# Mixture parts of a macaron block: gates of later blocks over the partitions by DMA through DRAM, rows normalised a block sooner

## The chip, the cores and the metric

One core of one Trainium2 chip runs the whole kernel. The time is the device time of an execution in microseconds (us). TensorE (PE) multiplies, VectorE (DVE), ScalarE (ACT) and GpSimd (POOL) do the rest, and SyncE (SP) issues all DMAs, in order.

## The reference, cut to what matters

The input x has 4 x 1024 rows of 256. Three sublayers follow each other: half a mixture, an attention with its own MLP, and half a mixture again with the same weights.

```python
x = x + 0.5 * _L0_ffn_ref(_layernorm(x), ...)
x = x + _L0_attn_ref(_layernorm(x), ...)
x = x + 0.5 * _L0_ffn_ref(_layernorm(x), ...)

def _L0_ffn_ref(x, gate_W, W1, b1, W2, b2, Ws1, bs1, Ws2, bs2, route_scale):
    scores = sigmoid(x @ gate_W) * route_scale
    topk_scores, topk_idx = top_k(scores, 2)
    topk_w = topk_scores / topk_scores.sum(-1, keepdims=True)
    gate_full = einsum('bsk,bske->bse', topk_w, one_hot(topk_idx, 8))
    h = gelu(einsum('bsd,edh->bseh', x, W1) + b1, approximate=False)
    y = einsum('bseh,ehd->bsed', h, W2) + b2
    shared = gelu(x @ Ws1 + bs1, approximate=False) @ Ws2 + bs2
    return einsum('bse,bsed->bsd', gate_full, y) + shared
```

There are 8 experts of width 128 and one shared one of the same width. Every expert is computed for every row; the gate multiplies its hidden layer.

## The kernel before, in words

The program has four parts: f (first mixture, and behind it the rows z for the attention, normalised twice and transposed, and the attention's weights, split in two), a (attention), m (the attention's MLP) and g (second mixture). f and g come out of one function, `ffn_phase`, with `tail` true for f. Each product in full precision is made of three of a high and a low part (`hi` on ACT rounds, `lo` on DVE takes what is left).

Both mixtures take the 4096 rows in NB = 8 blocks of BT = 512 (NT = 4 tiles of 128). The engines run their own lists in order, written out by hand in `body(i, par, first, last)` of each engine, and meet at counting semaphores. A block is a loop over e = 0 to 8, the steps: step 0 is the shared expert, steps 1 to 8 the gated ones. In a step

- PE makes the first layer (`first_layer`, L855, six products into `hid`), the gate product (`gate`, L873: `sel` picks one row of the transposed gates `gst` and spreads it over 128 partitions into `gbc`), and the second layer of the expert two steps back (`second_layer`, L896, twelve products into `acc`; at the first of a block also four products with the biases, L888);
- ACT makes the Gelu (`act_out`, L469), then `hi` of the expert before (L461);
- DVE makes `gated` = gate x `act_out` (`gating`, L670), then `lo` of the expert before (L676).

Between these stand, in block i, the pieces for block i + 1: statistics of its rows (`x_stats`), POOL's reciprocal root (`x_rstd`), `x_norm` to `xn`, its transposes (PE, L822, into the bank `aux`), `xt_hi` and `xt_lo`, the logits (L832), `neg_logits`, POOL's power for the sigmoid (`expneg`, L552), `choices` (the two largest) and `gates`, which lay the gates out in `gpad`. `gates_up` transposes `gpad` (L842) at step 0 of the next block, and `gate_stack` copies it into `gst`. In f there is also the work on the rows z of block i - 1: `z_stats` and `zz_stats` on DVE, two chains on POOL (`z_rstds`, L535 to L548), `z_norm` (L407, after step 4's Gelu) and `zn_norm` on ACT, transposes on PE, `zt_hi` and `zt_lo`.

In block 0 of f, ACT and DVE also split the attention's weights (`qkv_hi`, `qkv_lo`) into one buffer, `qkv_s`; SP stores it (`store_qkv`) before the next pair may be written. The code of block i on SP loads the rows for the residual, stores the results of block i - 1, loads the rows of block i + 2 and stores z of block i - 1.

## Time and profile before

| | |
|---|---|
| three runs | 2463.77, 2451.25, 2459.19 us; median 2459.19 |
| the profiled execution | 2457.1 us, span 2454.2 us |
| busy in the span | PE 98%, DVE 76%, ACT 69%, POOL 61% |
| f | from 0 to some 287 us |
| g | from some 2196 us to the end |
| mean granted clock of PE | 0.996 of 2.4 GHz |

The profile records one execution. The span is from its first to its last instruction; the execution's own time is 2.9 us more. Busy time of PE counts pipelined products, so what it waits for is read from its timeline, not from its share.

### The profile page before, as it was taken

The numbers are of one execution on the slowest core, as the hardware profiler recorded it, in microseconds if no ns is written. First come the engines' busy times: TensorE is split into PE (matmuls) and PEld (weight loads), VectorE is DVE, ScalarE is ACT, GpSimd is POOL, SyncE is SP. The second block draws the span as 40 slices with busy tenths as digits, with TensorE's granted clock in tenths as the row PEclk, the third lists the DMA queues.
The fourth block names the chain that finished last, engine by engine and source line by source line (L and its number), as shares of the span: only waits on it lengthen the run. The fifth ranks groups of instructions, "written<-read, shape, count | busy, mean of one in ns | idle before, by whom it ended". The sixth has DMA issues, their size and how long they took to land.

```text
span 2454.2 us, 46643 instructions
## 1 busy us (share of the span) xinstructions
PE 2405.0 (98%) x14568; PEld 2087.9 (85%) x14568; DVE 1862.3 (76%) x3599; ACT 1686.6 (69%) x2920; POOL 1505.2 (61%) x1536
## 2 busy tenths in 40 slices
PE   8999889999999999999999999999999999999999
PEld 7888778888888888888888888888888879988888
DVE  7777677878878788887878878788887865556665
ACT  4555577878778787777878778787877864543333
POOL 1333277787777777767777777777768754542220
PEclk9999999999999999999999999999999999999999
DMA  5422531223212132221213312132221345331111
GB/s 204 172 102 94 181 112 44 87 68 96 95 40 89 45 101 71 75 95 43 86 60 100 97 35 94 43 98 73 77 95 43 108 169 171 122 130 34 46 51 43
DMA packets 128311, 220.16 MB, mean 90 GB/s; under 512 B 6810, under 2 KB 89652, under 8 KB 119476
## 3 DMA queue, kind: packets, MB, share of 16 engines
q1 hardware_dynamic: 128180, 218.78, 27.6%
q8 instruction: 37, 0.61, 0.1%
q14 instruction: 94, 0.77, 0.1%
HBM read 114.95 MB, written 53.48 MB: 69 GB/s over the span
## 4 chain that ended last, share of the span: by engine, by line
PE 81%; DVE 8%; issue 6%; POOL 2%; ACT 2%; DMA 1%; SPq 0%; DVEq 0%; ACTq 0%; POOLq 0%
PE a_ov L1622 19%; PE a_sc L1586 18%; PE a_tr L1598 18%; PE a_pj L1541 7%; PE a_pj L1550 4%; PE g_acc L896 3%; PE g_hid L855 3%; PE f_acc L896 3%; PE f_hid L855 2%; PE m_proj L2025 1%; POOL m_zin L1877 1%; PE m_hid L2091 1%; DVE f_hp L676 1%; DVE g_hp L676 1%; PE g_aux L832 1%
## 5 line engine op out<-in xcount | busy, mean ns | idle before, releaser
L1498 DVE TENSOR_REDUCE a_nmax<-a_sc 128x1 f32<-128x1024 f32 x512 | 626.8, 1224 | 260.3 <-PE a_sc L1586 252.1
L1425 POOL TENSOR_SCALAR a_pr<-a_pr,a_rden 128x1024 f32<-128x1024 f32 x512 | 575.1, 1125 | 256.2 <-DVE a_rden L1503 185.7
L1341 ACT ACTIVATE a_pT<-a_tr 128x512 fp32r<-128x512 f32 x1024 | 559.8, 596 | 205.5 <-PE a_tr L1598 197.2
L1509 DVE TENSOR_TENSOR a_pT<-a_tr,a_pT 128x512 fp32r<-128x512 f32 x1024 | 650.1, 677 | 17.7 <-ACT a_pT L1341 17.7
L1622 PE MATMUL a_ov<-a_pT,a_v_s 128*128 128x512 f32 x2048 | 600.2, 415 | 3.1 <-DVE a_half L1489 2.0
L1347 ACT ACTIVATE a_pr<-a_sc,a_nmax 128x1024 f32<-128x1024 f32 x512 | 573.5, 1120 | 31.8 <-DVE a_nmax L1498 28.2
L1586 PE MATMUL a_sc<-a_k_s,a_q_s 128*128 128x512 f32 x2048 | 554.1, 392 | 3.4 <-DMA a_k_s<-a_k_s 3.4
L1598 PEld LDWEIGHTS a_tr<-f_ident,a_pr 128*128 128x128 f32 x4096 | 473.0, 140 | 93.6 <-DVE a_pT L1509 18.8
L1598 PE MATMUL a_tr<-f_ident,a_pr 128*128 128x128 f32 x4096 | 537.8, 273 | 9.8 <-DVE a_pT L1509 9.6
L1586 PEld LDWEIGHTS a_sc<-a_k_s,a_q_s 128*128 128x128 f32 x2048 | 380.0, 188 | 83.7 <-DMA a_k_s<-a_k_s 3.6
L1622 PEld LDWEIGHTS a_ov<-a_pT,a_v_s 128*128 128x128 f32 x2048 | 347.5, 189 | 54.3 <-issue 4.9
L1541 PE MATMUL a_pj<-a_z_s,a_wqk_s 128*128 128x512 f32 x756 | 193.6, 391 | 2.5 <-issue 2.2
L1541 PEld LDWEIGHTS a_pj<-a_z_s,a_wqk_s 128*128 128x128 f32 x756 | 141.6, 188 | 34.9 <-issue 3.3
L1302 ACT ACTIVATE a_staged<-a_pj,f_bias 128x512 f32<-128x512 f32 x126 | 86.8, 689 | 93.8 <-PE a_pj L1541 77.4
L469 ACT ACTIVATE g_act_out<-g_hid,f_b 128x512 f32<-128x512 f32 x72 | 49.6, 688 | 144.5 <-PE g_hid L855 144.5
L896 PEld LDWEIGHTS f_acc<-f_w2p,f_hp 128*128 128x128 f32 x864 | 114.0, 193 | 11.1 <-DVE f_hp L676 6.3
L469 ACT ACTIVATE f_act_out<-f_hid,f_b 128x512 f32<-128x512 f32 x72 | 49.2, 684 | 107.0 <-PE f_hid L855 107.0
L896 PE MATMUL f_acc<-f_w2p,f_hp 128*128 128x256 f32 x864 | 117.5, 286 | 4.5 <-DVE f_hp L676 3.9
L896 PEld LDWEIGHTS g_acc<-g_w2p,g_hp 128*128 128x128 f32 x864 | 112.1, 190 | 8.2 <-DVE g_hp L676 2.9
L896 PE MATMUL g_acc<-g_w2p,g_hp 128*128 128x256 f32 x864 | 115.5, 283 | 1.3 <-DVE g_hp L676 0.9
L855 PE MATMUL f_hid<-f_xT,f_w1p 128*128 128x512 f32 x432 | 115.7, 404 | 0.0
L855 PE MATMUL g_hid<-g_xT,g_w1p 128*128 128x512 f32 x432 | 113.1, 397 | 0.0
(222 smaller groups left out, 3260.0 us busy)
## 6 DMA issues: line engine op xcount, KB each, us to landing
a_z_s<-zT SPq DMA_DIRECT2D x32, 1024.0 KB, 7.8
a_k_s<-a_k_s SPq DMA_DIRECT2D x62, 512.0 KB, 5.7
a_wqk_s<-w_split SPq DMA_DIRECT2D x64, 256.0 KB, 3.2
a_v_s<-a_v_b SPq DMA_DIRECT2D x16, 1024.0 KB, 4.6
att<-a_ao SPq DMA_DIRECT2D x32, 512.0 KB, 2.9
m_in<-att SPq DMA_DIRECT2D x16, 1024.0 KB, 6.1
a_wv_s<-w_split SPq DMA_DIRECT2D x17, 512.0 KB, 3.8
zT<-f_zT SPq DMA_DIRECT2D x8, 1024.0 KB, 3.9
```

Source lines behind the costliest of these rows:

```text
L469: act.activation(act_out[:, e % 3], hid[:, (par + e) % 2], ACT.Gelu, bias=b1[:, weights_of(e):weights_of(e) + 1]).then_inc(s["gelu"], 1)
L855: o = pe.matmul(hid[:, (par + e) % 2], w1p[:, a, (c * NE + x) * HID:(c * NE + x + 1) * HID], xT[:, par, c, b], start=(n == 0), stop=(n == 5))
L896: o = pe.matmul(acc[:, t], hp[:, e % 3, a, t * P:(t + 1) * P], w2p[:, b, x * D:(x + 1) * D], start=False, stop=(e == NE - 1 and (a, b) == ...
L1341: act.activation(pT[:, (u // 4) % 2, 0, 4 * part:4 * part + 4, (u % 4) * P:(u % 4 + 1) * P], tr[:, part].rearrange("p (t q) -> p t q", t=4 ...
L1347: act.activation(pr[:, k % NP], sc[:, k % 2], ACT.Exp, bias=nmax[:, k % NP:k % NP + 1], accum_out=den[:, k % NP:k % NP + 1]).then_inc(s["e ...
L1425: pool.tensor_scalar(pr[:, k % NP], pr[:, k % NP], rden[:, k % NP:k % NP + 1], 1.0, ALU.mult, ALU.mult).then_inc(s["normed"], 1)
L1498: dve.tensor_reduce(nmax[:, k % NP:k % NP + 1], sc[:, k % 2], AX.X, ALU.max, negate=True).then_inc(s["negmax"], 1)
L1509: dve.tensor_tensor(to[:, 1], tr[:, part].rearrange("p (t q) -> p t q", t=4), to[:, 0].bitcast(F32), ALU.subtract).then_inc(s["tr_lo"], 1)
L1541: o = pe.matmul(bank[:], wqk_s[:, "QK".index(kind), c, a], z_s[:, c * 2 + b, part], start=(i == 0), stop=(i == 5))
L1586: o = pe.matmul(sc[:, k % 2, kb * BT:(kb + 1) * BT], q_s[:, slot, head, tile * P:(tile + 1) * P], k_s[:, slot, head, a, kb * BT:(kb + 1) * ...
L1598: o = pe.transpose(tr[:, part, j * P:(j + 1) * P], pr[:, (k - LAG) % NP, (4 * part + j) * P:(4 * part + j + 1) * P], ident[:])
L1622: o = pe.matmul(ov[:], v_s[:, vslot, kt, 2 * vhead:2 * vhead + 2] .rearrange("p k f -> p (k f)"), pT[:, blk % 2, a, kt], start=(kt == 0 an ...
```

## The change

It touches `ffn_phase` (both f and g). For blocks 1 to 7 the gate product is gone. `gpad` gets a fourth copy, of the unrounded gates at columns 64 to 71 (`EXACT`); after the transposes ACT copies these eight rows to `gf`, SP stores them to DRAM (`gate_rows`), waits for that, and loads them back spread over all partitions into `gB`, in two halves of four experts. `gating` reads `gB` there. Block 0 is gated as before.

For that, the gates of block i + 1 are ready within block i: from block 1 on the transposes of the rows stand in step 0 and the logits in step 1 (both in the free bank `gbc`), neg in step 2, choices in step 4, gates in step 5, `gates_up` in step 6, the copies in step 7 (tables `STEADY` and `FIRST`); and the rows of block i + 2 get their statistics in step 7 and are normalised in step 8. On POOL `expneg` comes ahead of both z chains. In f the rows of block 1 are loaded in the prologue and share a semaphore with the selector and the bias rows. Some semaphores are merged in the other parts, which leaves their orders as they were.

```diff
+    STEADY = dict(up_x=0, logits=1, neg=2, choices=4, gates=5, up_gates=6, gf=7, stack=7)
+    FIRST = dict(norm=2, up_x=3, logits=4, neg=5, choices=7, gates=7, up_gates=8, gf=8, stack=8) if tail else \
+        dict(stats=0, norm=1, up_x=2, logits=3, neg=4, choices=6, gates=7, up_gates=8, gf=8, stack=8)
...
+        def gates_across(i, counts):
+
+            copied, out, used = counts
+            half = E // 2
+            sp.wait_ge(s["gf"], copied)
+            sp.dma_start(gate_rows, gf[EXACT:EXACT + E]).then_inc(s["gates_out"], 16)
+            sp.wait_ge(s["gates_out"], out)
+            for h in range(2):
+                if h == 1:
+
+                    sp.wait_ge(s["gated"], used)
+                sp.dma_start(gB[:, h * half:(h + 1) * half].rearrange("p e t -> p (e t)"),
+                             gate_rows[h * half:(h + 1) * half].rearrange("e t -> (e t)").unsqueeze(0).partition_broadcast(P))\
+                    .then_inc(s["gates_in%d" % h], 16)
...
             if tail and has(i, -1):
                 store_z(i - 1, z_to)
+            if has(i, 1):
+                gates_across(i, counts)
...
+        def gate_copy(i, first):
+            act.wait_ge(s["gT_ps"], i + 1)
+            if not first:
+
+                act.wait_ge(s["gates_out"], (i - 1) * 16)
+            act.activation(gf[EXACT:EXACT + E], up_bank(first)[EXACT:EXACT + E, 0], ACT.Identity).then_inc(s["gf"], 1)
...
         def body(i, par, first, last):
-            if not last:
-                x_rstd(i + 1)
-            if tail and not first:
-                z_rstds(i - 1, 0)
+            if first and not tail:
+                x_rstd(1)
             if not last:
                 expneg(i + 1)
             if tail and not first:
+                z_rstds(i - 1, 0)
                 z_rstds(i - 1, 1)
+            if has(i, 2):
+                x_rstd(i + 2)
...
+        def gating(i, e, first):
             dve.wait_ge(s["gelu"], i * NE + e + 1)
-            dve.wait_ge(s["gbc"], i * E + e)
-            dve.tensor_tensor(gated[:, e % 3], gbc[:, (e - 1) % 2], act_out[:, e % 3],
-                              ALU.mult).then_inc(s["gated"], 1)
+            if first:
+                dve.wait_ge(s["gbc"], e)
+                gate = gbc[:, (e - 1) % 2]
+            else:
+                dve.wait_ge(s["gates_in%d" % ((e - 1) // (E // 2))], i * 16)
+                gate = gB[:, e - 1]
+            dve.tensor_tensor(gated[:, e % 3], gate, act_out[:, e % 3], ALU.mult).then_inc(s["gated"], 1)
...
         def gate(i, e, par, first):
 
-            if shared(e):
+            if shared(e) or not first:
                 return
```

SP's list at the end of block 0 of f, before (`w_split` is the store of the attention's weights, twice):

```order
L294 DMA f_qkv_in<-in_w_qkv 128x2048
L297 DMA f_xin<-in_x 128x4x256 [waits f_xn]
L360 DMA f_xres<-in_x 128x4x256
L366 DMA f_xin<-in_x 128x4x256 [waits f_xn]
L372 DMA w_split<-f_qkv_s 128x4096 [waits f_qkv_lo] x2
L360 DMA f_xres<-in_x 128x4x256 [waits f_res]
```

and now:

```order
L316 DMA f_qkv_in<-in_w_qkv 128x2048
L392 DMA f_xres<-in_x 128x4x256
L398 DMA f_xin<-in_x 128x4x256 [waits f_xn]
L364 DMA f_gate_rows<-f_gf 8x512 [waits f_gf]
L370 DMA f_gB<-f_gate_rows 128x2048 [waits f_gates_out]
L370 DMA f_gB<-f_gate_rows 128x2048 [waits f_gated]
L406 DMA w_split<-f_qkv_s 128x4096 [waits f_qkv_lo] x2
L392 DMA f_xres<-in_x 128x4x256 [waits f_res]
```

The three DMAs of the gates, the first and the second with waits of their own, have come ahead of both stores of the weights.

POOL's list in one block of the loop of f, before (`f_rs` is of the rows x, `f_zrs` and `f_zshift` of the rows z, `f_nl` is the power):

```order
L536 TENSOR_SCALAR f_rs<-f_mv 128x4 [waits f_stats]
L538 TENSOR_TENSOR f_rs<-f_rs,f_mhalf 128x4 [waits f_veps]
L532 ISA
L535 TENSOR_SCALAR f_zshift<-f_zmv 128x4 [waits f_z_stats]
L536 TENSOR_SCALAR f_zrs<-f_zmv 128x4
L538 TENSOR_TENSOR f_zrs<-f_zrs,f_mhalf 128x4 [waits f_z_veps]
L548 TENSOR_TENSOR f_zshift<-f_zshift,f_zrs 128x4 [waits f_z_rs]
L552 TENSOR_TENSOR f_nl<-f_ebase,f_nl 128x32 [waits f_neg]
```

and now:

```order
L595 TENSOR_TENSOR f_nl<-f_ebase,f_nl 128x32 [waits f_neg]
L575 ISA
L578 TENSOR_SCALAR f_zshift<-f_zmv 128x4 [waits f_z_stats]
L579 TENSOR_SCALAR f_zrs<-f_zmv 128x4
L581 TENSOR_TENSOR f_zrs<-f_zrs,f_mhalf 128x4 [waits f_z_veps]
L591 TENSOR_TENSOR f_zshift<-f_zshift,f_zrs 128x4 [waits f_z_rs]
L575 REGISTER_ALU
```

The power has gone from behind the first z chain to the head of the block; the rows of x have gone to its end.

PE's list in steps 6 and 7 of the loop of f now (`f_gpad` is what DVE's gate arithmetic writes):

```order
L919 MATMUL f_hid<-f_xT,f_w1p 128x512 [waits f_gelu]
L919 MATMUL f_hid<-f_xT,f_w1p 128x512 x5
L961 MATMUL f_acc<-f_w2p,f_hp 128x256 [waits f_h_lo]
L961 MATMUL f_acc<-f_w2p,f_hp 128x256 x11
L906 MATMUL f_gbc<-f_ident,f_gpad 128x128 [waits f_gpad]
L906 MATMUL f_gbc<-f_ident,f_gpad 128x128 x3
```

The transposes of the gates stood in step 0 of the next block, behind the whole block's other work.

## Rows read from the trace of the kernel before

**Rows 1.** Timeline of PE in f: start, us, line, operation, tile, count, idle before.
```profile
88.67 0.66 PE L842 MATMUL f_aux<-f_ident,f_gpad 128*128 128x128 f32 x4
...
101.86 1.63 PE L855 MATMUL f_hid<-f_xT,f_w1p 128*128 128x512 f32 x6
103.32 0.39 PE L873 MATMUL f_gbc<-f_gst,f_sel 128*128 128x512 f32 x1
103.55 1.59 PE L896 MATMUL f_acc<-f_w2p,f_hp 128*128 128x256 f32 x12
...
106.37 0.39 PE L873 MATMUL f_gbc<-f_gst,f_sel 128*128 128x512 f32 x1
...
121.22 0.65 PE L842 MATMUL f_aux<-f_ident,f_gpad 128*128 128x128 f32 x4 [0.20 <-DVE f_zT L718]
```

**Rows 2.** Timeline of PE in g.
```profile
2261.73 0.66 PE L842 MATMUL g_aux<-f_ident,g_gpad 128*128 128x128 f32 x4 [0.40 <-DVE g_gpad L661]
...
2293.44 0.66 PE L842 MATMUL g_aux<-f_ident,g_gpad 128*128 128x128 f32 x4 [0.39 <-DVE g_gpad L661]
```

**Rows 3.** Timeline of POOL in the same block of f.
```profile
103.12 0.20 POOL L535 TENSOR_SCALAR f_zshift<-f_zmv 128x4 f32<-128x4 f32 x1 [9.32 <-DVE f_zmv L581]
...
106.03 5.43 POOL L552 TENSOR_TENSOR f_nl<-f_ebase,f_nl 128x32 f32<-128x32 f32 x1 [1.02 <-DVE f_nl L610]
111.54 0.73 POOL L535 TENSOR_SCALAR f_zshift<-f_zmv 128x4 f32<-128x4 f32 x1
```

**Rows 4.** Timeline of ACT in the same block.
```profile
105.12 2.08 ACT L407 ACTIVATE f_zz<-f_res,f_zshift,f_zrs 128x256 f32<-128x256 f32 x4 [0.39 <-POOL f_zshift L548]
```

**Rows 5.** Timeline of DVE in the same block.
```profile
107.89 0.69 DVE L670 TENSOR_TENSOR f_gated<-f_gbc,f_act_out 128x512 f32<-128x512 f32 x1 [1.94 <-ACT f_act_out L469]
108.50 0.68 DVE L676 TENSOR_TENSOR f_hp<-f_gated,f_hp 128x512 fp32r<-128x512 f32 x1
109.10 1.40 DVE L576 BATCH_NORM_STATS2 f_zst<-f_zz 128x6 f32<-128x256 f32 x4
...
110.95 0.67 DVE L670 TENSOR_TENSOR f_gated<-f_gbc,f_act_out 128x512 f32<-128x512 f32 x1
...
114.68 0.17 DVE L627 TENSOR_SCALAR f_sg<-f_nl 128x32 f32<-128x32 f32 x1
...
117.05 0.69 DVE L670 TENSOR_TENSOR f_gated<-f_gbc,f_act_out 128x512 f32<-128x512 f32 x1 [0.21 <-DVE f_idx L636]
...
118.25 0.16 DVE L643 TENSOR_TENSOR f_ws<-f_top 128x4 f32<-128x4 f32 x1
...
120.41 1.28 DVE L718 TENSOR_TENSOR f_zT<-f_aux,f_zT 128x512 fp32r<-128x512 f32 x2
```

**Rows 6.** DMA issues: count, KB each, median us from issue to landing.
```profile
w_split<-f_qkv_s SPq DMA_DIRECT2D x3, 2048.0 KB, 6.5
...
z<-f_zz SPq DMA_DIRECT2D x8, 512.0 KB, 2.9
...
w_kept<-f_w2p SPq DMA_DIRECT2D x1, 2304.0 KB, 15.2
```

**Rows 7.** Timeline of PE in the last block of f.
```profile
271.91 2.38 PE L896 MATMUL f_acc<-f_w2p,f_hp 128*128 128x256 f32 x12 [2.63 <-DVE f_hp L676]
```

**Rows 8.** Timeline of PE at the start of block 1 of f.
```profile
52.78 0.66 PE L842 MATMUL f_aux<-f_ident,f_gpad 128*128 128x128 f32 x4 [1.99 <-DVE f_gpad L661]
...
57.04 2.77 PE L896 MATMUL f_acc<-f_w2p,f_hp 128*128 128x256 f32 x12
```

**Rows 9.** Timeline of ACT in the prologue and at the end of block 0.
```profile
12.35 0.42 ACT L501 ACTIVATE f_b2s<-f_b_in 128x256 fp32r<-128x256 f32 x1
...
47.46 2.18 ACT L431 ACTIVATE f_qkv_s<-f_qkv_in,f_ln 128x1024 fp32r<-128x1024 f32 x2
```

**Rows 10.** Timeline of DVE in the prologue.
```profile
12.01 1.29 DVE L601 TENSOR_TENSOR f_xT<-f_aux,f_xT 128x512 fp32r<-128x512 f32 x2 [2.23 <-ACT f_xT L442]
```

**Rows 11.** A window: busy time of PE, PEld, DVE, ACT, POOL, then PEclk.
```profile
54.00:61.00 7.00, 5.84 (x21) 4.67 (x20) 5.63 (x14) 1.21 (x2) 1.26 (x2) 0.51 0.71 301
```

More of the change, by code:

```diff
@@ L258, in ffn_phase, with now, has, up_bank @@
     SUMS_AT = {4: 0, 6: 1, 7: 2}
-    def later(first):
-        return 2 if tail and first else 0
+    STEADY = dict(up_x=0, logits=1, neg=2, choices=4, gates=5, up_gates=6, gf=7, stack=7)
+    FIRST = dict(norm=2, up_x=3, logits=4, neg=5, choices=7, gates=7, up_gates=8, gf=8, stack=8) if tail else \
+        dict(stats=0, norm=1, up_x=2, logits=3, neg=4, choices=6, gates=7, up_gates=8, gf=8, stack=8)
+    def now(what, e, first):
+        return (FIRST if first else STEADY).get(what) == e
+    def has(i, ahead=0):
+        return not isinstance(i, int) or 0 <= i + ahead < NB
+    def up_bank(first):
+        return aux if first else gbc
     def over_blocks(eng, body):
         body(0, 0, True, False)
-        with eng.Fori(0, (NB - 2) // 2) as it:
+        with eng.Fori(0, (NB - 4) // 2) as it:
             body(it * 2 + 1, 1, False, False)
             body(it * 2 + 2, 0, False, False)
+        body(NB - 3, 1, False, False)
+        body(NB - 2, 0, False, False)
         body(NB - 1, 1, False, True)
@@ L319, in rows_ahead @@
             sp.dma_start(xin[:, 0], rows_of(src, 0)).then_inc(s["x_in"], 16)
-        def has(i, ahead=0):
-            return not isinstance(i, int) or 0 <= i + ahead < NB
         def fixed(i):
@@ L474, in body @@
                     hi(i - 1, E, False)
-                if e == 2 + later(first) and not last:
-                    xt_hi(i + 1, 1 - par)
+                if now("up_x", e, first) and not last:
+                    xt_hi(i + 1, 1 - par, up_bank(first))
+                if now("gf", e, first) and not last:
+                    gate_copy(i + 1, first)
                 if e == 4 and tail and not first:
@@ L793, in body @@
                 if not last:
-                    if e == 7 + later(first) // 2:
+                    if now("choices", e, first):
                         choices(i + 1)
+                    if now("gates", e, first):
+                        gates(i + 1)
+                    if now("stack", e, first):
+                        gate_stack(i + 1, 1 - par, up_bank(first))
+                if has(i, 2):
+                    if e == 7:
+                        x_stats(i + 2, par)
                     if e == 8:
-                        gates(i + 1)
+                        x_norm(i + 2, par, False)
                 if tail and not first and e == 8:
@@ L865, in gate @@
                 pe.wait_ge(s["gst"], i + 1)
-                if tail and first:
-                    pe.wait_ge(s["sel"], 1)
+                if tail:
+                    pe.wait_ge(s["rounded"], 2)
             if tail and first and e == 2:
                 pe.wait_ge(s["bias"], 2)
-            if e >= 3 or not first:
-                pe.wait_ge(s["gated"], i * E + e - 2)
+            if e >= 3:
+                pe.wait_ge(s["gated"], e - 2)
             pe.matmul(gbc[:, (e - 1) % 2], sel[:, (e - 1) * P:e * P], gst[:, par],
@@ L945, in body @@
                     second_layer(i - 1, E - 1 + e, 1 - par, False)
[L946 to L950 removed]
                 if not last:
[L952 to L956 removed]
+                    if now("up_x", e, first):
+                        if not first:
+                            pe.wait_ge(s["gated"], i * E)
+                            pe.wait_ge(s["gst"], i + 1)
+                            pe.wait_ge(s["gf"], i)
+                        transposes(i + 1, xn, s["xn"], s["xT_ps"], up_bank(first))
+                    if now("logits", e, first):
+                        logits(i + 1, 1 - par, up_bank(first))
+                    if now("up_gates", e, first):
+                        gates_up(i + 1, up_bank(first))
                 if e == 8 and tail and not first:
[L958 to L960 removed]
+                    pe.wait_ge(s["zT_lo"], i * DC)
                     transposes(i - 1, zn, s["zn"], s["zT_ps"])
```

150 lines of the change are left out of this document (78 added, 72 removed).

## Prediction

> **What bounds the kernel now.** I looked first at the two mixture parts alone, since nothing else changes, and there at PE in order of time [rows 1, 2]. In a block of the first part (f) PE goes from group to group without a gap: the transposes of the gates come at 88.67 and again at 121.22, and of these 32.55 us 0.20 are idle. Between two gate products (103.32 and 106.37) lie 3.05 us, and the product itself holds PE for 0.23 (103.32 to 103.55). I call the nine turns of the loop over experts steps 0 to 8. A step without its gate product is 2.82 us of PE. In the second part (g) a block takes 31.70 us (2261.73 to 2293.44), with 0.40 idle. So PE is the bound of both parts, and 2 x 7 blocks x 8 products x 0.23 = 25.8 us is all that the removal can give.
>
> Then I looked at who could be next. The reader is to see three things: POOL's power for the sigmoid takes 5.43 us [rows 3]; ACT's normalisation of z sits between two Gelus and once waited 0.39 us for POOL [rows 4]; and DVE works through its list in order, with statistics and the gate arithmetic between the products [rows 5]. They have slack today because the pow starts at step 4 and the gates are wanted only in the next block.
>
> **The change part by part.** The times are those of the one profiled execution: span 2454.2, its own time 2457.1, which lies 2.1 below the median 2459.19.
>
> *Removed:* per later block 8 x 0.23 = 1.84 us of PE.
>
> *Added on DVE, ACT and by DMA.* One copy into gpad (0.1, from the gate arithmetic of 2.16 us being thirteen small instructions [rows 5]). One ACT copy of the gates, in step 7, when ACT is half idle. The store of 16 KB and two broadcasts of 1024 KB have until the next block's step 1 (three steps, some 9 us). No row shows a broadcast of that size. From below it is a 512 KB store, 2.9 us; from above a queue of three stores whose last landed after 15.2 [rows 6]. I take 2.9 for the store of the gates and 4.5 for a half, between 2.9 for 512 KB and 6.5 for 2048 KB: hidden, with about 1.5 us to spare.
>
> *The f loop, moved waits.* Logits now come in step 1, so the pow starts in step 2; POOL has it ahead of both z chains, where before the first z chain was ahead. Worked from the PE start of step 2 as zero:
> - In the trace the pow starts 4.17 after the PE group of its step (101.86 to 106.03) [rows 1, 3]. It ends at 4.17 + 5.43 = 9.60.
> - The z chain takes 2.00 from its start to ACT's start (103.12 to 105.12) [rows 3, 4]. It would then run beside DVE's two-input products. The second z chain did so too, and its first instruction took 0.73 in place of 0.20. So 2.5, and ACT begins z at 12.1.
> - From there to the gated product of step 5 it is 2.77 (105.12 to 107.89), to the low part 0.61, and 0.68 to its end [rows 4, 5]: the second layer of step 4 may start at 16.2. PE is there after step 2 (2.82, and 0.5 for four bias products, a third of twelve in 1.4), three steps (8.46) and a first layer (1.4): 13.2. It waits 3.0.
> - DVE is free at 16.1, makes the statistics of z (1.85, from 109.10 to 110.95) and the gates (2.16 + 0.1) [rows 5]: gpad at 20.3. PE has been ready since 16.2 + 1.4 = 17.6 and waits 2.7.
>
> PE's own work in a block is 32.5 - 0.5 of waits - 1.84 = 30.1; with 5.7 of waits 35.8. The low end of the z chain (2.0) and of the handovers gives 34.9. I take 35.5, that is +3.0 over 32.5, for the six blocks between block 1 and block 7: **+18** (15 to 20). Block 7 has no pow; its own z wait (2.63 idle [rows 7]) takes up what its gate products free: 0.
>
> *f, block 0 to 1.* SP issues in order. The store of the first split attention weights now stands behind the copy, the store and both broadcasts of the gates, and ACT waits for its landing before it rounds the next pair. In the trace the gates of block 1 reached PE at 52.78, and ACT's pair began at 47.46 with no wait [rows 8, 9]. After: one step sooner, 2.2 later (below): 52.0; ACT's copy until 53.1; the gate store 2.9 to 56.0; both halves and the weights' store issued by 56.8. 2048 KB alone took 6.5, 5120 KB queued took 15.2 from the last issue [rows 6]: for 4096 KB some 11.7, landing at 68. ACT's pair 2.1, Gelu and rounding 1.2, DVE's low part 0.8: the last product of block 0 starts at 72.2 instead of 57.04 [rows 8]. Less the 2.2 that is counted next: **+13** (11 to 18).
>
> *Prologue.* DVE now takes the statistics of block 1 ahead of splitting xT, and they wait for a semaphore that block 1's rows, the bias rows and the selector share. Today the bias rows were rounded at 12.35 and xT split at 12.01 [rows 9, 10]. 512 KB more ahead and 1.8 us of statistics make it 0 to 3.6 later: **+2.2**.
>
> *Clock.* After a wait of 1.99 at 52.78 PE's granted clock was 0.51 for 7 us, half of 2.4 GHz, and after one of 2.63 a group of twelve took 2.38 us instead of 1.59 [rows 1, 7, 8, 11]. Two waits within 4.5 us in each of six f blocks are at least as long. I take 1.7 for each block (twice 0.8) and 0.6 more where PE has stood for 13 us: **+10.8** (0 to 15).
>
> *g.* No z chain. Zero is the PE start of step 4: the low part of step 3 is issued by 3.6 (4.17 less neg and the handover, some 0.5), the choices take 2.37 (114.68 to 117.05 [rows 5]), two products 1.2, the gates 2.25: their transposes at 9.5, where PE comes at 8.7. With that 0.8, some 0.2 at the second layer and 0.5 for the rows' transposes: 31.7 - 0.4 - 1.84 + 1.5 = 30.95. Six blocks by 0.75 and eight products of the last: **-6** (-9 to -3).
>
> Sum: 18 + 13 + 2.2 + 10.8 - 6 = +38. 2457 + 38 = **2495**.
>
> **A rule weighed.** Two-input products with both inputs in SBUF are eight more per block now (gB and act_out). In the trace such a product (108.50, gated and hp) took 0.68 us in the middle of the pow, which ran from 106.03 for 5.43 [rows 3, 5]: it wasn't held up. The Trainium skill, "SBUF — State Buffer", section "SBUF: two separate sides", says that VectorE with two SBUF inputs and GpSimd lock a shared port pair for a whole instruction, and that the other blocks fully. By it each pow would hold the product of step 3 until it ends; the trace agrees for the short POOL instruction only (0.73 for 0.20) and not for the pow.
>
> **The rivals.**
> - *Same waits, clock holds* (0.25). The two falls in the rows stand behind waits of 1.99 and 2.63; that is little to foretell six blocks by, and PE's waits here are of 3.0 and 2.7 with a busy group of 1.4 between. 2495 - 10.8 = 2484.
> - *The gates come too late by DMA* (0.08). A broadcast reads the same 8 KB for all 128 partitions. If a half took 12 us, step 1's product would be 6 late, some 4 of it on PE, in 13 blocks: 2495 + 52 = 2547. It decides from about 6.5 us a half. Beside it: the Trainium skill, "DMA: Bandwidth & Descriptors", section "Why a DMA increments its semaphore by 16 and not by 1", lets the two outermost sizes set how many engines share a DMA; both are 128 here, so by it all 16 do. No run here shows it.
> - *The pow holds the port* (0.03). A gated product held until the pow ends costs some 3 us more a block in f, 1.5 in g: 2495 + 27 = 2522. Against it stands the product at 108.50. This is the rule of the Trainium skill's page on SBUF above.
> - *The other side: PE stays the only bound* (0.08). The place is POOL in step 4. If z's chain is ready when ACT gets there, about 5 us sooner than by my sum, neither wait arises, nor the clock's falls: 14 blocks by -1.84, with 13 + 2.2 + 0.6 from the start: 2457 - 25.8 + 15.8 = 2447. If the weights' store isn't waited for either: 2434. Against it: the 5.43 us of the pow.
> - *The change doesn't do its work* (0.02): a part of the gate products stays, and the waits come all the same: 2500.
>
> The forecast itself has 0.54.
>
> **How the numbers follow.** The range must hold the forecast and its clock rival: from 2484 less the low ends (hold-up 2, loop 3, prologue 2) to 2495 with the high ends of hold-up and clock: 2477 to 2508. That leaves out 0.19. A change within 0.5% (12 us) can't be told from none here: the three runs lie 12.5 us apart. Faster by more has 0.04, within 0.04, slower 0.92.
>
> **What would show it.** Right: the period between gate transposes in f about 35.5, with two PE waits in it (second layer for the low part, transposes for gpad) of 2 to 3 us each, and z's normalisation on ACT with some 2 us of idle before it put down to POOL; a PE gap of 12 to 14 us near 60; in g 30.9 per block; PE's clock at half after the waits; half a broadcast landing within 5 us. Wrong: no idle before z, or a PE gap near 60 below 5 us, or gated products that wait for gB.

## The result

| | before | after |
|---|---|---|
| median, us | 2457.49 (4 runs, 2451.25 to 2463.77) | 2501.86 (4 runs, 2498.53 to 2506.25) |
| span of the profiled execution | 2454.2 | 2504.5 |
| mean granted clock of PE | 0.996 | 0.984 |

The ratio is 1.0182, 95% interval 1.0149 to 1.0214: 44 us slower. The profiled execution of the changed kernel is the slowest of its four, so the two traces differ by 50.3 us of span, and the accounts below are made on them.

Where the time went is read from marks that both traces have. The timeline of PE in the kernel before, at the first product of block 1, of block 7, of the attention and of g:

```profile
53.19 2.10 PE L855 MATMUL f_hid<-f_xT,f_w1p 128*128 128x512 f32 x6
...
251.54 1.64 PE L855 MATMUL f_hid<-f_xT,f_w1p 128*128 128x512 f32 x6
...
286.69 1.55 PE L1541 MATMUL a_pj<-a_z_s,a_wqk_s 128*128 128x512 f32 x6
...
2196.45 2.91 PE L855 MATMUL g_hid<-g_xT,g_w1p 128*128 128x512 f32 x12
```

The same four products after the change:

```profile
55.45 1.64 PE L919 MATMUL f_hid<-f_xT,f_w1p 128*128 128x512 f32 x6
...
294.19 1.64 PE L919 MATMUL f_hid<-f_xT,f_w1p 128*128 128x512 f32 x6
...
333.08 1.55 PE L1605 MATMUL a_pj<-a_z_s,a_wqk_s 128*128 128x512 f32 x6
...
2249.86 2.92 PE L919 MATMUL g_hid<-g_xT,g_w1p 128*128 128x512 f32 x12
```

| stretch | before | after | difference |
|---|---|---|---|
| prologue and block 0 of f | 53.19 | 55.45 | +2.3 |
| blocks 1 to 6 of f | 198.35 | 238.74 | +40.4 |
| block 7 of f | 35.15 | 38.89 | +3.7 |
| attention and its MLP | 1909.76 | 1916.78 | +7.0 |
| g | 257.75 | 254.64 | -3.1 |

Block 1 of f, PE [rows 8 show the same place before]:

```profile
55.04 0.66 PE L906 MATMUL f_aux<-f_ident,f_gpad 128*128 128x128 f32 x4 [2.69 <-DVE f_gpad L710]
...
75.80 2.93 PE L961 MATMUL f_acc<-f_w2p,f_hp 128*128 128x256 f32 x12 [12.93 <-DVE f_hp L732]
...
89.19 1.60 PE L961 MATMUL f_acc<-f_w2p,f_hp 128*128 128x256 f32 x12
```

The row at 75.80 is the last product of block 0. What held it, on ACT and on SP:

```profile
55.73 0.59 ACT L483 ACTIVATE f_gf<-f_aux 8x512 f32<-8x512 f32 x1 [3.79 <-PE f_aux L906]
71.48 2.19 ACT L465 ACTIVATE f_qkv_s<-f_qkv_in,f_ln 128x1024 fp32r<-128x1024 f32 x2 [15.15 <-DMA w_split<-f_qkv_s]
```

```profile
56.35 0.30 SPq L364 DMA_DIRECT2D f_gate_rows<-f_gf  x1
57.82 0.81 SPq L370 DMA_DIRECT2D f_gB<-f_gate_rows  x2
58.67 0.43 SPq L406 DMA_DIRECT2D w_split<-f_qkv_s  x1
```

The weights' store goes out at 58.67, behind three DMAs of the gates, and ACT waits for it until 71.48. PE stands for 12.93 us at the last product of block 0, and its products then take 2.93 us in place of 1.60 until some 88. The granted clock from 76 to 88 is 0.51, its lower level.

The loop of f, PE in blocks 2 to 4 (the gate transposes once a block):

```profile
137.12 1.69 PE L961 MATMUL f_acc<-f_w2p,f_hp 128*128 128x256 f32 x12 [2.52 <-DVE f_hp L732]
141.17 0.66 PE L906 MATMUL f_gbc<-f_ident,f_gpad 128*128 128x128 f32 x4 [2.37 <-DVE f_gpad L710]
...
143.67 2.49 PE L961 MATMUL f_acc<-f_w2p,f_hp 128*128 128x256 f32 x12
...
177.84 0.66 PE L906 MATMUL f_gbc<-f_ident,f_gpad 128*128 128x128 f32 x4 [2.36 <-DVE f_gpad L710]
...
179.72 1.59 PE L961 MATMUL f_acc<-f_w2p,f_hp 128*128 128x256 f32 x12
...
213.17 1.12 PE L906 MATMUL f_gbc<-f_ident,f_gpad 128*128 128x128 f32 x4 [2.27 <-DVE f_gpad L710]
```

Two waits in every block from 1 to 6, the first of 2.3 to 2.6 us (for the low part), the second of 2.1 to 2.6 (for `gpad`). From 177.84 to 213.17 it is 35.33 us, a block in which the clock held (the second layer behind the waits takes 1.59); from 141.17 to 177.84 it is 36.67, with a fall (2.49). The block of the first row, on POOL, DVE and ACT:

```profile
125.30 5.43 POOL L595 TENSOR_TENSOR f_nl<-f_ebase,f_nl 128x32 f32<-128x32 f32 x1 [11.15 <-DVE f_nl L658]
130.82 0.47 POOL L578 TENSOR_SCALAR f_zshift<-f_zmv 128x4 f32<-128x4 f32 x1
```

```profile
126.90 0.69 DVE L727 TENSOR_TENSOR f_gated<-f_gB,f_act_out 128x512 f32<-128x512 f32 x1 [1.68 <-ACT f_act_out L510]
...
129.67 0.38 DVE L626 BATCH_NORM_AGGREGATE f_zmv<-f_zst 128x2 f32<-128x6 f32 x4 [0.16 <-DVE f_zst L621]
```

```profile
133.09 2.08 ACT L441 ACTIVATE f_zz<-f_res,f_zshift,f_zrs 128x256 f32<-128x256 f32 x4 [2.88 <-POOL f_zshift L591]
```

The z chain starts at 130.82, right behind the power; but the statistics that it needs were only finished at 130.05. With POOL free it could have started 0.77 sooner and no more. With the statistics sooner and the power where it is, it could not have started before 130.73, the power's end, either. Each of the two alone holds z here. Block 7 has no power, and still ACT idles ahead of z, and PE waits 3.84 us and runs at half speed behind it:

```profile
311.74 2.08 ACT L441 ACTIVATE f_zz<-f_res,f_zshift,f_zrs 128x256 f32<-128x256 f32 x4 [2.54 <-POOL f_zshift L591]
```

```profile
317.43 2.93 PE L961 MATMUL f_acc<-f_w2p,f_hp 128*128 128x256 f32 x12 [3.84 <-DVE f_hp L732]
```

The attention, whose orders the change leaves as they were, has a wait ahead of its first scores in both kernels. Before, on PE, the first group of scores and one some 32 us later:

```profile
298.27 1.19 PE L1586 MATMUL a_sc<-a_k_s,a_q_s 128*128 128x512 f32 x4 [3.38 <-DMA a_k_s<-a_k_s]
...
329.92 1.07 PE L1586 MATMUL a_sc<-a_k_s,a_q_s 128*128 128x512 f32 x4
```

After, the same two groups:

```profile
344.66 2.07 PE L1650 MATMUL a_sc<-a_k_s,a_q_s 128*128 128x512 f32 x4 [3.37 <-DMA a_k_s<-a_k_s]
...
384.79 1.07 PE L1650 MATMUL a_sc<-a_k_s,a_q_s 128*128 128x512 f32 x4
```

The first scores take 2.07 us in place of 1.19, and so it goes on for some 24 us at half speed: the granted clock is 0.88 from 336 to 436 us, and 1.00 from 290 to 390 in the kernel before. From the first of the two groups to the second it is 40.13 us instead of 31.65, so 8.5 us are lost there; 7.0 are left at the attention's end. That is all of the difference in this stretch.

In g, PE waits for `gpad`, for the low part and for `xn`:

```profile
2338.56 0.66 PE L906 MATMUL g_gbc<-f_ident,g_gpad 128*128 128x128 f32 x4 [0.54 <-DVE g_gpad L710]
2346.69 1.69 PE L961 MATMUL g_acc<-g_w2p,g_hp 128*128 128x256 f32 x12 [0.44 <-DVE g_hp L732]
...
2369.64 0.66 PE L906 MATMUL g_gbc<-f_ident,g_gpad 128*128 128x128 f32 x4 [0.54 <-DVE g_gpad L710]
2379.82 1.09 PE L886 MATMUL g_gbc<-f_ident,g_xn 128*128 128x128 f32 x8 [0.71 <-DVE g_xn L642]
```

A block takes 31.08 us there (2338.56 to 2369.64), 31.70 before [rows 2]. The broadcasts in f, by count, KB each and median us from issue to landing (in g it is 5.3 too):

```profile
f_gB<-f_gate_rows SPq DMA_DIRECT2D x14, 1024.0 KB, 5.3
```

### The profile page after: what moved, and what is told of

It reads as the page before. It is cut to its first block, busy times and chain, and to the rows that moved or that the text cites. A ratio compares the mean times of both kernels' runs of the same rounds, so it can differ in the third digit from the quotient of the medians.

```text
span 2504.5 us, 46233 instructions
## 1 busy us (share of the span) xinstructions
PE 2405.3 (96%) x14456; PEld 2087.4 (83%) x14456; DVE 1864.1 (74%) x3615; ACT 1695.1 (68%) x2934; POOL 1513.3 (60%) x1536
## 4 chain that ended last, share of the span: by engine, by line
PE 77%; DVE 7%; issue 7%; POOL 4%; ACT 2%; DMA 2%; SPq 0%; DVEq 0%; ACTq 0%; POOLq 0%
PE a_ov L1686 19%; PE a_sc L1650 18%; PE a_tr L1662 18%; PE a_pj L1605 7%; PE a_pj L1614 4%; PE g_hid L919 3%; PE g_acc L961 2%; PE f_hid L919 2%; PE f_acc L961 1%; POOL f_nl L595 1%; POOL m_zin L1941 1%; PE m_hid L2155 1%; PE m_proj L2089 1%; DVE a_pT L1573 1%; DMA w_split<-f_qkv_s 1%
## 5 line engine op out<-in xcount | busy, mean ns | idle before, releaser
L961 PE MATMUL f_acc<-f_w2p,f_hp 128*128 128x256 f32 x864 | 122.6, 294 | 34.4 <-DVE f_hp L732 34.2
L919 PE MATMUL f_hid<-f_xT,f_w1p 128*128 128x512 f32 x432 | 121.3, 419 | 0.0
```

Of the source, the lines that this page charges most:

```text
L919: o = pe.matmul(hid[:, (par + e) % 2], w1p[:, a, (c * NE + x) * HID:(c * NE + x + 1) * HID], xT[:, par, c, b], start=(n == 0), stop=(n == 5))
L961: o = pe.matmul(acc[:, t], hp[:, e % 3, a, t * P:(t + 1) * P], w2p[:, b, x * D:(x + 1) * D], start=False, stop=(e == NE - 1 and (a, b) == ...
```

## The experiments

Each is the changed kernel with one edit or with a few. Ratios are to the kernel before on the same chip; the changed kernel's is 1.0182.

| edit | median, us | ratio, 95% interval |
|---|---|---|
| weights' store first | 2483.8 | 1.0106 (1.0079 to 1.0134) |
| first z chain ahead of the power | 2525.2 | 1.0274 (1.0245 to 1.0303) |
| z's statistics in step 1, chain ahead | 2483.9 | 1.0108 (1.0081 to 1.0135) |
| gates ahead of the second statistics | 2492.5 | 1.0152 (1.0128 to 1.0175) |
| the last two together | 2475.4 | 1.0082 (1.0063 to 1.0101) |
| PE's waits in f's loop filled | 2493.6 | 1.0146 (1.0123 to 1.0169) |
| prologue's statistics later | 2500.7 | 1.0176 (1.0156 to 1.0195) |
| gates 5 us late by DMA | 2521.5 | 1.0253 (1.0222 to 1.0285) |
| four edits | 2463.8 | 1.0016 (1.0001 to 1.0031) |
| four edits, rows sooner | 2480.4 | 1.0097 (1.0078 to 1.0117) |
| waits filled, the attention's too | 2490.8 | 1.0131 (1.0110 to 1.0153) |
| four edits, rows sooner in g, filled | 2458.4 | 0.9996 (0.9983 to 1.0010) |

**The hold-up.** SP's order in block 0 alone:

```diff
+            if tail and isinstance(i, int) and i == 0:
+                store_qkv(0)
             if has(i, 1):
                 gates_across(i, counts)
...
         body(0, 0)
         if tail:
-            store_qkv(0)
             store_qkv(1)
```

> One edit to the changed kernel: in block 0 of f, SP stores the first split attention weights ahead of the store and the two broadcasts of the gates. Theory (the hold-up is SP's order and the queue of 4096 KB behind it): the store goes out some 8 us sooner and lands before ACT's next pair wants the buffer, so the idle of 12.9 us before the second layer at 75.80 shrinks to 1 us or less, and the clock does not fall behind it (75.8 to 87.8 ran at half, some 6 us): 2502 - 12 - 6 = 2484. Rival (the queue itself is the limit: broadcasts and store share the DMA engines and land together whatever the order): ACT still waits 5 us or more, 2494 or slower.

2483.8, where the theory had 2484. The store goes out at 43.79, 14.9 us sooner, where some 8 were expected. ACT's pair, and PE's next second layer:

```profile
54.95 2.19 ACT L466 ACTIVATE f_qkv_s<-f_qkv_in,f_ln 128x1024 fp32r<-128x1024 f32 x2
```

```profile
56.66 2.43 PE L962 MATMUL f_acc<-f_w2p,f_hp 128*128 128x256 f32 x12 [0.46 <-DVE f_hp L733]
```

ACT starts the pair 16.5 us sooner and waits for nothing; at the last product of block 0 PE waits 0.51 us instead of 12.93. Blocks 1 to 6 take 221.10 us (first products at 54.05 and 275.15) instead of 238.74, with falls of the clock in the same four blocks. So the hold-up with its clock is 17.6 us, 12.4 of it that wait and the other 5, by the rows, nearly all the clock behind it.

**What makes z late.** POOL's order alone:

```diff
         def body(i, par, first, last):
+            if tail and not first:
+                z_rstds(i - 1, 0)
             if not last:
                 expneg(i + 1)
             if tail and not first:
-                z_rstds(i - 1, 0)
                 z_rstds(i - 1, 1)
```

> One edit: in the loop of f POOL has the first z chain ahead of the power again, as before the change. Theory of the prediction (the power at the head of POOL's list is what makes z late): the idle before z's normalisation on ACT falls from 2.9 us to 0.5 or less, PE's wait for the low part goes, some 2.5 a block: 2502 - 15 = 2487. Rival, read from the trace of the changed kernel: z's statistics on DVE end at 130.05, only 0.8 before POOL was free anyway, so the order is worth 1.1 us; and the power then ends at 137.4 instead of 130.7, DVE holds gated 5 behind choices that wait for it until 139.8 instead of 135.8: 4 us more a block in six blocks, 2502 + 24 = 2526.

2525.2, where the rival had 2526. PE, POOL and ACT:

```profile
144.01 2.93 PE L962 MATMUL f_acc<-f_w2p,f_hp 128*128 128x256 f32 x12 [7.25 <-DVE f_hp L733]
```

```profile
132.41 0.43 POOL L578 TENSOR_SCALAR f_zshift<-f_zmv 128x4 f32<-128x4 f32 x1 [16.20 <-DVE f_zmv L627]
134.83 5.43 POOL L595 TENSOR_TENSOR f_nl<-f_ebase,f_nl 128x32 f32<-128x32 f32 x1
```

```profile
134.99 2.08 ACT L441 ACTIVATE f_zz<-f_res,f_zshift,f_zrs 128x256 f32<-128x256 f32 x4 [2.62 <-POOL f_zshift L591]
```

With POOL idle for 16.20 us ahead of the chain, ACT still waits 2.62 for it (2.88 with the power in front). What POOL waits for is DVE's statistics. And the power, now later, holds the choices on DVE and with them the gated product of step 5: PE waits 7.25. With the statistics in step 3 the order that I had named as the cause is the better of the two. The run shows that the order alone doesn't free z; it doesn't show that the power would be harmless with the statistics out of the way.

**z's statistics sooner.** With the same order on POOL, and on DVE:

```diff
-                    if e == 3:
+                    if e == 1:
                         z_stats(i - 1)
```

> The statistics of z go from step 3 to step 1 on DVE (right behind the residual), and POOL has the first z chain ahead of the power. Theory (z is late because its statistics stand at the end of step 3 with 2.8 us to the next step, and the power in front of the chain): the chain is done before the power starts, ACT normalises z without idle, the low part's wait of 2.5 on PE goes in all six blocks, the wait for gpad stays at about 2: 2502 - 15 = 2487, and 2480 if the clock falls go too. Rival (DVE's list is full there, so gated products of steps 2 and 3 come late and PE waits at those): 2498 to 2506, with new waits for the low part in steps 3 and 4.

2483.9, 3 us under the theory's first figure.

```profile
124.65 2.07 ACT L441 ACTIVATE f_zz<-f_res,f_zshift,f_zrs 128x256 f32<-128x256 f32 x4
```

```profile
130.06 1.70 PE L962 MATMUL f_acc<-f_w2p,f_hp 128*128 128x256 f32 x12 [0.92 <-DVE f_hp L733]
134.11 0.97 PE L907 MATMUL f_gbc<-f_ident,f_gpad 128*128 128x128 f32 x4 [2.35 <-DVE f_gpad L711]
```

z's normalisation waits for nothing. The low part's wait is 0.92, not 0: the choices still stand ahead of the gated product of step 5 on DVE, and wait 0.78 for the power there. The wait for `gpad` has not moved. This run has two edits. The statistics in step 1 with the power still at the head of POOL's list was not run; by the changed kernel's rows the chain would have begun at 130.73 at the earliest, some 0.1 sooner than it did.

**The wait for gpad.** In step 5 DVE makes the gates first:

```diff
                         z_stats(i - 1)
-                    if e == 5:
-                        zz_stats(i - 1)
...
                     if now("gates", e, first):
                         gates(i + 1)
+                if tail and not first:
+                    if e == 5:
+                        zz_stats(i - 1)
```

> One edit: in step 5 of f's loop DVE makes the gates ahead of the second statistics of z. Theory (PE's wait for gpad is DVE's order behind gated 5): gpad comes 1.9 us sooner, the wait of 2.4 falls to 0.5, the wait of 2.5 for the low part stays: 2502 - 6 x 1.9 = 2491, some 4 less if fewer clock falls follow. Rival (the second z chain becomes late: its normalisation in step 7 waits, and the transposes of step 8 with it): a new wait of 2 us on ACT and PE near the end of each block, and 2500 or slower.

```profile
134.83 0.66 PE L908 MATMUL f_gbc<-f_ident,f_gpad 128*128 128x128 f32 x4 [0.54 <-DVE f_gpad L710]
137.87 1.70 PE L963 MATMUL f_acc<-f_w2p,f_hp 128*128 128x256 f32 x12 [0.99 <-DVE f_hp L732]
```

2492.5, near the 2491 expected, but only in part as reasoned: the wait for `gpad` falls from 2.37 to 0.54 (that for the low part stays, 2.51), and 0.99 comes back one group later, at the low part that DVE makes behind the gates. A block without a fall takes 34.6 (gate transposes at 100.22, 134.83 and 169.42), 0.7 less than 35.33. In six blocks that is some 4.4 of the 9.4 us, where 11 were expected. Most of the rest is, by the two profiles, the clock: here it holds in the first blocks of the loop, and the attention takes 1913.3 us instead of 1916.8. The wait for `gpad` is DVE's order.

**Both.**

> The two edits in f's loop together: statistics of z in step 1 with the first z chain ahead of the power, and the gates ahead of the second statistics. Theory (two waits in series, each with its own cause on DVE, POOL and ACT): both waits of a block are gone but for some 0.5, its period falls from 36.6 to 30.6 us: 2502 - 6 x 4.4 - 7 for the clock = 2469. Rival (the gates of a step 6 are simply too early for the chain logits, power, choices, gates: with one wait gone the other grows): a wait of over 1.5 us stays before the transposes of gpad, 2480 or slower.

2475.4: between the two, and the rival's wait of over 1.5 us is not there. The waits left are the 0.92, 0.53 and 0.99 of the two runs above, the period is 33.0 (gate transposes at 131.50, 164.50 and 197.50), and PE's clock is 1.00 from 100 to 300.

**The clock alone.** Work in place of idle time, into the bank `aux`:

```diff
+        def fill(i, n):
+
+            pe.wait_ge(s["zT_lo"], i * DC)
+            for t in range(n):
+                pe.transpose(aux[:, 0, 0:P], ident[:], ident[:])
...
+                if tail and not first and not last and e == 6:
+                    fill(i, 16)
```

> PE does 16 transposes of the identity into an unused bank ahead of each of the two waits in step 6 of f's blocks 1 to 6 (2.1 us each, work that takes the place of idle time; waits and orders stay). Theory (a clock fall of some 1.7 us follows in four of these blocks because PE stood): the granted clock stays near 1.0 in the loop, each period is 35.3 us: 2502 - 7 = 2495. Rival (the falls have another cause, such as the 13 us stand near 60, and come all the same): 2502, or 2504 with the transposes running over the end of the waits.

2493.6, the theory's 2495. Windows of the changed kernel and of this one (the stretch, busy PE, PEld, DVE, ACT, POOL, then PEclk):

```profile
100.00:200.00 100.00, 88.04 (x567) 79.78 (x568) 70.34 (x226) 47.30 (x84) 27.82 (x29) 0.95 0.57 208
```

```profile
100.00:200.00 100.00, 96.64 (x667) 88.30 (x666) 73.16 (x236) 48.11 (x85) 30.73 (x31) 1.00 0.56 206
```

The waits end when they did, the clock stays up, and a block takes 35.3 to 35.6 us each time (gate transposes at 138.90, 174.26, 209.60). In the changed kernel the blocks with a fall took 36.7 to 37.1. So a fall in the loop costs 1.3 to 1.7 us, and with the waits filled it doesn't come. Why it comes behind these waits in four blocks of six and not in the other two, no run shows. The times alone don't prove the gain: the interval overlaps the changed kernel's.

**The prologue.**

```diff
-            x_stats(1, 1)
             xt_lo(0, 0)
             dve.wait_ge(s["w_hi"], 1)
             dve.tensor_tensor(w1p[:, 1], w1_in[:], w1p[:, 0].bitcast(F32), ALU.subtract).then_inc(s["w_lo"], 1)
+            x_stats(1, 1)
```

> One edit: in the prologue the statistics of block 1 stand behind the split of xT and of the first layer's weights on DVE. Theory (the wait for the semaphore shared with bias rows and selector, and 1.8 us of statistics, delay block 0 by 2.2): block 0 starts 2 us sooner, 2500. Rival (the first layer's weights or the choices end last there, so the statistics cost nothing): 2502.

2500.7. The intervals overlap, so the times don't tell the two apart. The traces do in part: the first gate transposes behind block 0 come at 52.49 here, and at 53.26 to 55.04 in the changed kernel and the six others above, which have its prologue. That is 0.8 to 2.6 us.

**Gates late by DMA.** The first half is loaded, waited for, and loaded again, then the second:

```diff
-            for h in range(2):
+            for n, h in enumerate((0, 0, 1)):
+                if n == 1:
+                    sp.wait_ge(s["gates_in0"], once)
```

> The first half of the gates is broadcast twice, one after the other has landed, so both halves come 5.3 us later than now, in f and g. Theory (now hidden with 3.5 us to spare in f and 5 in g, read from the changed trace as landing against the first gated product): the products of step 1 come 2 us late in f and 0.5 in g, PE waits 1 to 2 a block: 2502 + 7 x 1.5 + 2 = 2515. Rival (DVE and PE already wait for the gates now, hidden in other waits): each block 5 us longer, 2570.

2521.5: 20 us for 14 blocks by some 5 us of delay. Neither figure was met, the theory's is nearer. DVE's waits for a broadcast in g (us in total, times, the longest):

```profile
DVE g_gated L729 <- DMA g_gB<-g_gate_rows: 21.0, 7, 5.1
```

In f it is 11.4 us in 6. That is 3.0 a wait in g and 1.9 in f, so some 2 to 3.5 us were to spare. Read directly in the changed kernel it is 3.4 in f (a half issued at 147.21, 5.3 to its landing, its first gated product at 155.95) and 2.9 in g (2312.62 and 2320.85), not the 5 that I had read there. The changed kernel, which has no such wait, had hidden its broadcasts.

**Four edits together** (store, statistics of z, gates, prologue):

> The four edits that gave time together: the weights' store ahead of the gates on SP, the statistics and first chain of z sooner, the gates ahead of the second statistics of z, the prologue's statistics later. Theory (hold-up, loop and prologue are independent terms): 2502 - 18 (first) - 26.5 (both in the loop) - 1 = 2456, the same as before the change. Rival (the waits overlap, or the time given back is taken by the clock in the attention's first 25 us, whose products ran at half speed in the changed kernel): 2465 or slower.

2463.8, ratio 1.0016: some 8 over the theory, at the rival's edge. The loop is as in the pair (33.0), f ends at 291.80. The attention's first projection behind the 3.36 us of wait:

```profile
304.40 2.54 PE L1618 MATMUL a_pj<-a_wv_s,a_z_s 128*128 128x256 f32 x12
```

The fall again: from the first projection to g's first product it is 1916.2 us here, 1909.8 in the profile before. That stretch, in which no edit lies, took 1909.1 to 1918.0 in the profiles of the changed kernel and of the eleven others without fill in it. Eleven of these twelve have a fall there, all but the kernel before. By the granted clock it is some 20 to 24 us long in the nine where the stretch is 1913 or more, and under 10 us in the two where it is 1909.1 and 1912.3.

The lists of executions agree, for the kernel before too. Of the seventeen of it that were run beside the last kernel of this section, eight have a mean granted clock of 0.996 or more and took 2450.6 to 2456.4 us, nine have 0.992 to 0.994 and took 2458.4 to 2466.1. Of the twelve of the four edits, five have 0.996 or more (2453.7 to 2461.1) and seven have less (2463.8 to 2467.9). So the 8 us over the theory fit how often the clock falls, and where it doesn't fall the kernel is about level with the kernel before. That these falls are the attention's is shown only for the executions with a profile.

**Rows sooner.** On the four edits:

```diff
-    STEADY = dict(up_x=0, logits=1, neg=2, choices=4, gates=5, up_gates=6, gf=7, stack=7)
+    STEADY = dict(up_x=0, logits=1, neg=2, choices=4, gates=5, up_gates=7, gf=7, stack=8)
...
-                    if e == 7:
+                    if e == (7 if first else 3):
                         x_stats(i + 2, par)
-                    if e == 8:
+                    if e == (8 if first else 7):
                         x_norm(i + 2, par, False)
```

with the second statistics of z in step 6, and on POOL the second z chain behind the reciprocal root of the rows of block i + 2.

> On top of the four edits, in the loops of f and g: the transposes of gpad a step later (7), the statistics of the rows of block i + 2 in step 3 instead of 7 and their normalisation in 7 instead of 8, the second statistics of z in step 6. Theory (DVE's work stands in steps 4 to 8, 18 us of it for 15 us of PE, while steps 0 to 3 have room): the waits for gpad (0.5), the low part behind it (1.0) and xn (0.7) go, 1.5 a block in f and 1.2 in g: 2456 - 9 - 7 = 2440, faster than before by 0.6%. Rival (the gates now reach gB too late for the first gated product of the next block): 2 us of wait at the second layer in step 2 or 3 of each block, 2460 or slower.

2480.4, where the theory had 2440: a miss, by neither mechanism. In block 2 of f, DVE:

```profile
118.30 1.41 DVE L623 BATCH_NORM_STATS2 f_st<-f_xin 128x6 f32<-128x256 f32 x4 [11.21 <-DMA f_xin<-in_x]
```

and SP's issues ahead of that load:

```profile
93.65 0.53 SPq L324 DMA_DIRECT2D w_kept<-f_w2p  x1
...
101.55 9.74 SPq L398 DMA_DIRECT2D f_xin<-in_x  x1
```

The rows' load stands once behind the stores of the kept weights [rows 6]; wanted in step 3 it isn't in time, and PE stands 10.8 us for it. In each f block from 1 on the transposes of z also wait 1.7 to 2.0 for a second chain that is now late; which of its two delays, DVE's or POOL's, does it was not tested. In g, where neither exists, the waits for `gpad` and `xn` go and others of some 0.4 stay: g takes 249.8 us instead of 254.6, 4.8 of the 7 foretold.

**More fill.** 24 transposes in f's last block too, and 24 ahead of the attention's first scores, into its bank `tr`:

```diff
-                if tail and not first and not last and e == 6:
-                    fill(i, 16)
+                if tail and not first and e == 6:
+                    fill(i, 24 if last else 16)
...
             project(kind, part, n, True)
+        for _ in range(24):
+            pe.transpose(tr[:, 0, 0:P], ident[:], ident[:])
```

> The changed kernel with PE's waits filled with transposes as before (16 ahead of each wait in step 6 of f's blocks 1 to 6), and 24 more ahead of the wait in f's last block and ahead of the attention's first scores (3.84 and 3.37 us of idle). Theory (the attention's first 25 us ran at half speed because PE had stood, which cost some 9 us in the changed kernel and in some executions of others): 2494 - 8 = 2486 at most, and its executions lie closer together than the 12 us of the earlier filled kernel. Rival (that fall is not tied to the stand ahead of it): 2494, spread as before.

2490.8, between the two: the theory had 2486 at most. The interval overlaps the first fill's, and the four executions lie within 8.7 us, those of the first fill within 12.2. The attention's stretch is 1909.0 us in its profile, under each of the unfilled ones (1909.1 to 1918.0), though one of those came as low. The clock is at 1.00 for the 24 us from the first scores.

**The last kernel.** The four edits, `STEADY` as in the rows' run, the attention's fill, and

```diff
-                    if e == 7:
+                    if e == (7 if first or tail else 3):
                         x_stats(i + 2, par)
-                    if e == 8:
+                    if e == (8 if first or tail else 7):
                         x_norm(i + 2, par, False)
...
         over_blocks(pe, body)
+        if tail:
+            for _ in range(16):
+                pe.transpose(gbc[:, 0, 0:P], ident[:], ident[:])
         second_layer(NB - 1, E - 1, 1, False)
```

> The four edits of before, the transposes of gpad a step later in both parts, the rows of block i + 2 sooner in g alone (in f they waited once 11.2 us for a load that stood behind the kept weights), the second statistics of z left in step 5, and PE's waits ahead of the last second layers of f (16 transposes) and ahead of the attention's first scores (24) filled. Theory: from 2464, g gives 5 (its part took 249.8 in the kernel with the rows sooner, 254.6 in the changed one), f's loop 7 of the 9 us of waits for gpad and behind it, the clock 6: 2446, faster than before by 0.4%. Rival (the waits of f's loop only move to the transposes of z in step 8, and the fill gives nothing): 2458, the same as before.

```profile
118.94 1.70 PE L965 MATMUL f_acc<-f_w2p,f_hp 128*128 128x256 f32 x12 [2.19 <-DVE f_hp L734]
```

2458.4, ratio 0.9996: the rival's figure, no faster than before, though not by its mechanism. In f's loop the waits for `gpad` (0.53) and the low part behind it (0.99) became one of 2.19: putting PE's transposes later gives nothing where DVE makes the gates ahead of that low part. Blocks 1 to 6 got worse for it, g took 250.4, and the attention took 1908.6 with a fall of a few us at most (its clock is 0.93 for the 24 us from the first scores). Its twelve executions lie within 5.7 us, those of the four edits without fill within 14.3 (on another chip), those of before on that chip within 15.5. The four edits' f with this g was not tried.

## Why the prediction was right, and where it was not

The forecast was 2495 in a range of 2477 to 2508; it came to 2501.9, a difference of 44.4 on the medians where 38 was forecast. (The upper end of the range takes in the high ends of the loop and the prologue too; with the two that the text names it would be 2504.) Term by term, on the two traces, which differ by 50.3:

| term | predicted | measured |
|---|---|---|
| prologue | +2.2 | +2.3 |
| hold-up, with its clock | +13, +0.6 | +17.6 |
| six blocks of f | +18 | +17 |
| clock in them | +10.2 | +6 |
| block 7 of f | 0 | +3.7 |
| attention | 0 | +7.0 |
| g | -6 | -3.1 |

The sum came out partly by luck. The loop's and the hold-up's waits were right in place and near in size. But the clock behind the hold-up, block 7 and g were together 11 us too low, the clock in the loop was 4 too high, and the attention, at nothing in the forecast, makes 7 in this pair of executions. The kernel before has executions with the low clock too, so that 7 is not the change's own cost as far as the runs show.

- **Prologue.** 2.3 is the profiled execution, the slowest. Six other profiles with the same prologue have the gate transposes behind block 0 at 53.26 to 54.94, the kernel before at 52.78: 0.5 to 2.2.
- **Hold-up.** Shown by the run that moved one store. The mechanism is as worked out: SP's order, and ACT behind the landing. The 13 fits better than its working. The store went out at 58.67 and landed at some 71.5, 1.9 and 3.5 us later than foretold, and the last product of block 0 started at 75.80, not 72.2. Against that, the sum took all the time since 57.04 for loss, and some 4 us of it are PE's work that has moved ahead of this product: with the store first it starts at 61.97, 7.92 behind the first product of block 1 (3.85 before), with only 0.51 of wait. The two errors cancel. The clock behind it was mis-sized: 5 us, not 0.6.
- **The f loop.** The two waits (3.0 and 2.7 foretold, 2.5 and 2.4 found) and the period (35.5; 35.33 where the clock held) are right in place and size: 17 is six times 2.83. The reason that I gave for the first is half of it. I wrote that z comes late because the power has POOL ahead of the chain. It does hold the chain until 130.73, but taking it away alone gives 0.3 us of ACT's idle time, because a second cause holds z nearly as long. That is what no longer stands between step 3, where DVE makes z's statistics, and step 4, behind whose Gelu ACT wants the chain. In the kernel before, PE had the logits there:

```profile
100.15 1.85 PE L832 MATMUL f_aux<-f_gwp,f_xT 128*128 128x16 f32 x16
```

  They have gone to step 1, and each step is shorter by its 0.23 as well. From the statistics' end to ACT's being ready for z it was 1.8 us (102.92 to 104.73), and is 0.2 now (130.05 to 130.21). Of the 2.5 us that ACT idles more, 1.65 are this and 0.8 are the chain, which starts behind the power and runs slower. Block 7 of the kernel before, which has neither logits nor a power, has the wait already:

```profile
266.22 2.08 ACT L407 ACTIVATE f_zz<-f_res,f_zshift,f_zrs 128x256 f32<-128x256 f32 x4 [2.01 <-POOL f_zshift L548]
```

  Block 7 and the restored order show that z waits without the power ahead; the run with the statistics in step 1 and the chain ahead shows that with both causes gone it doesn't wait. Which share the logits' place has is read from the rows, not tested. The sum held by luck: the statistics' end (130.05) and the power's (130.73) happen to lie within 0.7 us.
- **Block 7.** The step "block 7 has no pow: 0" failed for the same reason: z is late there too, 3.84 in place of 2.63 [rows 7], and the clock falls behind it.
- **The second wait** is DVE's order, as written: 1.8 us less of it with the second statistics out of the way, of which 1.0 comes back at the low part.
- **Clock.** 1.7 for a block with a fall was the size (1.3 to 1.7), shown by the fill, but the fall came in four of six blocks: 6 in the loop, what is left of 40.4 - 17.6 - 17.0. What I missed is the fall in the attention, +7 in the profile. The rival in which the clock holds is out.
- **g.** The period of 30.95 is 31.1 to 31.35. The rest is mostly block 0, whose end I had not costed: 0.31, 0.98 and 0.61 of waits where the kernel before had none.
- **DMA.** 5.3 us a half (4.5 taken), 1.47 for the gates' store (issue at 56.35, broadcasts at 57.82; 2.9 taken), hidden with some 2 to 3.5 us to spare. The rival of late gates is out.
- **The port.** A gated product with both inputs in SBUF took 0.69 us at 126.90, in the middle of a power that ran from 125.30 for 5.43. It wasn't held. By the rule of the Trainium skill, "SBUF — State Buffer", section "SBUF: two separate sides", it would have been held until the power's end at 130.73; the trace doesn't agree with it for the power.

The 25.8 us of gate products are gone from PE, as read. Little of it arrived as time: in f two waits of 4.9 us a block took the 1.84, in g waits took all but 0.4 to 0.6 of it. With the orders mended the kernel is within 0.2% of where it was.

## What to carry to other kernels

Moving work between steps changes the distance between a producer's place and its consumer's, also for work that isn't moved: list what stood between them and what hides there now. Where a queue in order gets new entries with waits in them, look at every entry behind them for one that another engine waits for. When an engine that was the bound is relieved by little, look first whether its neighbours have the room in the very steps where the work is put; here, by its busy times, DVE had 18 us of work for 15 in steps 4 to 8, and room in 0 to 3 (five steps of 1.3 for gated and low part, choices 2.4, gates 2.25, statistics 1.85 twice, `gst` 0.7, `xn` 1.4, `zT` 1.3; against five of 2.82 and 1.2 of transposes).

## What was not expected of the hardware

A wait of 3.3 to 3.5 us ahead of the attention's first scores, the same in all kernels without fill there, is followed by half speed for 20 to 24 us in nine profiles, for under 10 us in two and not at all in one (1909 to 1918 us for the stretch). With most of the wait filled (1.1 us left of it), both profiles had 1909, and the last kernel's twelve executions lay within 5.7 us, where those of the kernel before lay within 15.5. Why the fall comes in one execution and not in another stays open.
